# Straight code in place of the hardware loops over pairs of heads in a vision block's attention

## The reference

```python
q = split_heads(x @ Wq, S); k = split_heads(x @ Wk, T); v = split_heads(x @ Wv, T)
attn = jnp.einsum('bhsd,bhtd->bhst', q, k) * scale + pos_bias
attn = jax.nn.softmax(attn, axis=-1)
out = jnp.einsum('bhst,bhtd->bhsd', attn, v)
...
h = h + out @ Wo
```

## Time and profile before

| | us |
|---|---|
| median of 3 runs | 3251.09 |
| the runs | 3235.87, 3251.09, 3252.10 |
| the profiled execution | 3249.65 |
| its span, first to last instruction | 3247.6 |
| PE busy in it | 2958.2 |
| ACT busy in it | 2710.2 |
| mean granted clock of PE | 0.946 |

### The profile page before, as it was taken

One profiled execution on the slowest core, in us unless ns is written; L12 is line 12 of the kernel. 1 busy time (PEld: TensorE's weight loads), 2 busy tenths in 40 slices (PEclk: granted clock), 3 DMA queues, 4 the chain that ended last, 5 costly groups with the idle time before them and its releaser, 6 DMA issues. The chain is left out here.

```text
span 3247.6 us, 60885 instructions
## 1 busy us (share of the span) xinstructions
PE 2958.2 (91%) x21844; PEld 876.1 (27%) x21844; DVE 635.7 (20%) x798; ACT 2710.2 (83%) x2867; POOL 763.8 (24%) x1420
## 2 busy tenths in 40 slices
PE   6949999999999999999999999999999996699999
PEld 3522222222222222222222222222222221255555
DVE  5730111111111111011111111111111111654441
ACT  4739998989898989898989898999989996376664
POOL 1222222322222222222223232323222231000000
PEclk9979999989999999999999999999999998799999
DMA  4440111111110111111010111011111100101100
GB/s 107 159 155 24 30 30 34 27 29 27 30 26 26 26 26 26 26 29 27 26 26 26 26 26 26 26 26 27 27 32 27 31 15 19 41 23 48 41 28 20
DMA packets 166132, 118.09 MB, mean 36 GB/s; under 512 B 111318, under 2 KB 156212, under 8 KB 165108
## 3 DMA queue, kind: packets, MB, share of 16 engines
q1 hardware_dynamic: 163780, 107.50, 12.1%
q0 software_dynamic: 2048, 6.43, 0.5%
HBM read 67.42 MB, written 47.75 MB: 35 GB/s over the span
## 5 line engine op out<-in xcount | busy, mean ns | idle before, releaser
L707 ACT ACTIVATE pr<-ps 128x1179 f32<-128x1179 f32 (+1 forms) x2176 | 2306.4, 1139 | 208.4 <-PE ps L650 171.3
L670 PE MATMUL ps<-pr,va 128*32 128x393 f32 x12800 | 1444.6, 524 | 0.0
L626 POOL TENSOR_TENSOR pr<-pr,e_cur 128x310 f32<-128x310 f32 (+19 forms) x1344 | 701.7, 532 | 1809.8 <-ACT pr L707 1806.8
L650 PE MATMUL ps<-qa,ka 48*128 48x393 f16 (+12 forms) x3808 | 719.6, 329 | 147.4 <-ACT pr L707 59.2
L647 PE MATMUL ps<-qa,ka 51*128 51x393 f16 (+18 forms) x3360 | 636.1, 320 | 36.3 <-ACT pr L707 21.7
L718 DVE COPY o_sb<-ps 128x393 f32<-128x393 f32 x64 | 36.4, 569 | 2239.3 <-PE ps L670 2239.3
L650 PEld LDWEIGHTS ps<-qa,ka 48*128 48x128 f16 x3808 | 193.5, 96 | 758.4 <-ACT pr L707 611.5
L670 PEld LDWEIGHTS ps<-pr,va 128*32 128x32 f32 x12800 | 255.5, 109 | 494.5 <-issue 387.4
L647 PEld LDWEIGHTS ps<-qa,ka 51*128 51x128 f16 (+1 forms) x3360 | 167.9, 95 | 729.4 <-ACT pr L707 713.3
L1402 PE MATMUL ps<-ln_all,w 128*128 128x393 f32 x512 | 181.8, 498 | 5.1 <-ACT hid L1462 5.1
L1462 ACT ACTIVATE hid<-ps,b 128x393 f32<-128x393 f32 x256 | 135.3, 587 | 56.6 <-PE ps L1402 56.1
(11 more groups left out here) (117 smaller groups left out, 930.9 us busy)
## 6 DMA issues: line engine op xcount, KB each, us to landing
qa<-q_halves SPq DMA_DIRECT2D x64, 196.5 KB
ka<-k_halves SPq DMA_DIRECT2D x64, 196.5 KB
att_rows<-o_norm SPq DMA_DIRECT2D x64, 196.5 KB, 2.5
ln_rows<-ln SPq DMA_DIRECT2D x32, 196.5 KB, 3.4
q_halves<-halves SPq DMA_DIRECT2D x32, 196.5 KB, 2.6
k_halves<-halves SPq DMA_DIRECT2D x32, 196.5 KB, 3.5
qa<-q_halves SPq DMA_DIRECT2D x64, 98.2 KB
ka<-k_halves SPq DMA_DIRECT2D x64, 98.2 KB
```

The source lines that it names most:

```text
L626: nc.gpsimd.tensor_tensor(p, p, e_cur[0:keys, par, t:t + z - a], ALU.mult).then_inc(s_band, 1)
L650: last = nc.tensor.matmul(out[:, cut:W], ka[r:r + 48, par, k0:k0 + keys], qa[r:r + 48, par, q0 + cut:q0 + W], start=True, stop=True, tile_ ...
L670: last = nc.tensor.matmul(ps[quad:quad + 32, O_PS + side, 0:W], va[0:keys, par, kt], pr[0:keys, g % SLOTS_PR, j], start=(kt == 0), stop=(k ...
L707: nc.scalar.activation(pr[:, g % SLOTS_PR, 0:m], ps[:, 3 * (g % 2):3 * (g % 2) + m, 0:W], ACT.Exp, scale=1.0 / (LIFT * LIFT)).then_inc(s_e ...
```

## The change

The loops of POOL, PE and ACT over k are now Python loops, so the instructions of all 16 pairs are written out one after the other, and every wait compares with a constant. The loops of DVE and SP stay hardware loops. In PE all 16 pairs are calls of `pair`; the order of instructions within them is the same. The test in `scores` is simpler because k is now always a number.

```diff
@@ gpsimd
-                with pool.Fori(0, NBH // 2) as k:
+                for k in range(NBH // 2):
                     for i, u in enumerate(banded):
@@ scores
-                    if not (isinstance(k, int) and k == 0 and g < AHEAD):
+                    if not (k == 0 and g < AHEAD):
                         pe.wait_ge(s_exp, k * NG + g - AHEAD + 1)
@@ tensor
-                with pe.Fori(0, NBH // 2 - 1) as k:
-                    pair(k, False)
-                pair(NBH // 2 - 1, True)
+                for k in range(NBH // 2):
+                    pair(k, k == NBH // 2 - 1)
@@ scalar
-                with act.Fori(0, NBH // 2) as k:
+                for k in range(NBH // 2):
                     for g in range(NG):
```

## The result

The changed kernel takes 3094.64 us (median of 4 runs, 3093.17 to 3101.1). The kernel before, in 4 runs beside it, takes 3244.79 us. The ratio is 0.9541 with a 95% interval of 0.9523 to 0.9558: faster by 4.6%, 150 us. The profiled execution took 3101.1 us, against 3249.65 before. The median lies at the low end of the range of the prediction, 3092 to 3158.

A forecast was written before the change was run, and what follows sets the result against it. The attention, three quarters of the time, was taken as bound by PE and ACT, both nearly full and handing work to each other. 3249.65 - 100.8 (edges) - 22 (ACT's waits) = 3126.9, given as 3126 us; range 3092 to 3158.

The forecast's parts named there:

- Edges: At the 15 passages from pair to pair: 312.62 us measured, less 15 x 14.12 for changes of head, 100.8 us gained.
- three parts: Edges of ACT, edges of PE and the clock behind the edges: 1.7, about 2.5 and 2.7 us an edge.
- PE's edge: PE's loop jump before a pair's sixth group: 14 taken edges go, each worth about 2.5 us.
- Edges of ACT: ACT's loop jump before a pair's first Exp: 15 taken edges go, at 1.7 us each, 25 us.
- ACT's waits: Exps waiting for scores: with constants 0.08 us less once in four groups, 43.5 us in full, half taken, 22 us.
- PE's waits: Constants instead of registers in PE's waits: nothing gained, since the last pair already has them and runs its middle equally long.
- POOL: POOL loses its loop edges and register work: nothing gained, hidden by the Exp and score stream.
- Dips: Granted clock halving at changes of head or side, 1.53 us each: 18 as before, so 0; ends -27 and +27 us.
- More code: Instruction fetching: loop bodies are too long to be kept, so straight code fetches the same amount; bytes about as before or fewer.
- The edge stays: Rival: something else at the change of pair costs, not the jump; edges keep 20.84 us, only waits gain, 3228; chance 0.03.
- fetching becomes the bound: Rival: straight code makes PE stop 2.2 us at each of 182 instruction packets, 400 us lost, 3526; chance 0.04.
- small branch cost: The skill page's some 0.11 us per compare-and-branch: 15 would be under 2 us, and the change would bring only the waits.

The follow-up runs named there:

- loops_swap: The kernel before, all loops kept, with the order of ACT's two waits turned round (s_pv first, s_score second): 3177.22 us, ratio 0.9806.
- pe_straight: The kernel before with only PE's loop written out, ACT's and POOL's loops kept: 3201.57 us, ratio 0.9871.
- pool_straight: The kernel before with only POOL's loop written out: 3237.42 us in one run.
- pe_straight_swap: The kernel before with PE's loop written out and ACT's two waits turned round (s_pv first, s_score second), ACT's and POOL's loops kept: 3096.62 us, ratio 0.9548.
- act_body_short: The kernel before, loops and wait order kept, without the 36 waits of ACT's body that repeat the count of the group before: 3217.06 us, ratio 0.9899.
- act_body_padded: pe_straight_swap with 34 more waits, fulfilled long ago, in ACT's loop body: 3181.71 us, ratio 0.9791.
- edge_alone: The changed kernel with two added loops of tiny copies behind ACT's last Exp, 6 turns of 8 and 5 of 600; read by its gaps, no total given.
- half_edges_swap: loops_swap with two pairs in each turn of the three loops, so PE jumps 6 times instead of 14: 3140.52 us, ratio 0.9683.
- pe_pause: The changed kernel with 150 already fulfilled waits (75 instructions) in PE where its loop's edge had been, each pair but the first: 3242.35 us, ratio 0.9991.
- straight_swap: The changed kernel with the order of ACT's two waits turned round (s_pv first, s_score second): 3123.32 us, ratio 0.9632.

## Why the prediction was right

- **Edges: right to 1 us.** 100.8 forecast by setting the measured stretch against its twin at the change of head, 101.0 found. Adding what each loop costs alone would have failed: the two share the time at the lower clock, 4.0 us for ACT's, 5.7 for PE's, 6.7 for both. The text's three parts do add up to the same 100.8, because the clock's part was taken as what is left. "PE's edge is worth about 2.5 us" holds only beside ACT's stop.
- **Edges of ACT: right, on thin ground.** The 1.7 us were real, and "the loop bodies are too long to be kept" was true of ACT's body by at most 36 instructions. The working behind it couldn't have told: with ACT's body kept, loops_swap still moves 3.33 + 0.20 MB, 59 bytes for each of its 60309 instructions, against 68 before. The stop is the price of that body's length and not of a loop.
- **ACT's waits: right in size, half right in reason.** 22 us forecast, 24.5 found. Half of 43.5 was a good choice: eight groups, in which ACT waits twice, take 22.71 x 8 / 21 = 8.65 us before and 8.56 after, so of two delays of 0.08 us one counts. The reason that the text gave for half was not tested. The rows named the true mechanism, but the text tied it to constants ("With constants all of them can be of the first kind"). Turning two lines round does the same, with loops, and with constants the turned order is slow again.
- **PE's waits and POOL: right.** pe_straight has the old middle, and the one run of pool_straight shows nothing.
- **Dips: the term that was mis-sized.** "I take 18 dips in all as before, so 0" was the step: there were 3 in all, and the 15 fewer are worth 22.8 us. Its stated end, none at all (-27 us), nearly happened. This is nearly the whole distance from 3126 to 3101 for the profiled execution. The timed median, 3094.6, is another 6 us lower. The low end of the range, 3092, was made of nearly the full value of the waits and 12 us of dips; it was the dips that came, so that the median lies inside it by 2.6 us owes something to luck.
- **More code: right.** The queues moved less, 2.87 + 0.54 MB against 4.16, and no new stops appeared.
- **The rivals.** "The edge stays" and "fetching becomes the bound" did not come. The small branch cost that would have made the first one true is real too, as the short loop shows, only not for a body that has to be fetched again.

What the change itself does is worth dividing: pe_straight_swap reaches 3096.6 us with PE alone written out and two lines of ACT turned round. Its ratio, 0.9548, can't be told from the changed kernel's 0.9541, and ACT's and POOL's loops are kept.

## What to carry to other kernels

Cost a loop edge by comparing the stretch across it with a stretch of equal work elsewhere, not by adding the stops. Put last, directly ahead of the instruction, the wait that really comes last where a register value is computed between two waits (and, with constants alone, first, as these kernels show); then look at where the row starts behind its releaser, since 0.08 us at every fourth hand-over, of which half counted, was 24 us here. And before writing a loop out, see by the instruction queue's packets whether its body is fetched again each turn: a few redundant waits can decide it.

## What the runs showed of the hardware

- ACT kept a loop body of 374 instructions and needed no fetch at its turns (25 packets in all on the smaller instruction queue in act_body_short and loops_swap). With 34 or 36 instructions more it fetched at its turns (100 packets in act_body_padded and the kernel before) and stood 1.7 to 2.0 us at the first of them.
- A turn of the loop of 8 copies cost at most 0.15 us; a turn of 600 copies 1.5 to 1.6 us of idle (edge_alone). PE's turn left ACT idle for 2.88 us with a body of one pair and for 2.65 with a body of two (the first turns of loops_swap and half_edges_swap), and each went with 2.1 to 2.5 packets more on PE's instruction queue.
- At an edge whose only stop was ACT's 1.69 us, PE's granted clock was 0.73 in the mean of the window (act_body_padded, first edge). Of the 4.3 us that such an edge cost, about 1.5 are the stop (1.69 against 0.21 us) and 2.8 the slower stretch behind it.
- An already fulfilled wait instruction took some 0.1 us of PE when 75 stood in a row (pe_pause, 7.66 us).
- Of two neighbouring waits with nothing between them, the instruction itself carries the first, and the second has an instruction of its own ahead of it. The semaphores in the trace's records of the changed kernel and of straight_swap show it, and so do the starts of the Exps: 0.03 us behind the scores when their wait stands first in straight code, 0.09 when it stands second. With a register value computed between the two, the Exp carries the second: 0.11 us when the scores' wait stands first.
